# Layer 2 as one loop of 64 state steps, with the products of a step shared out anew among four engines

## What is computed

```
xn = layernorm(x)
# s: selective state space; inner width 256, 16 states
x_main, z = split(xn @ W_in.T);  x_main = silu(conv3(x_main) + conv_b)
dt_raw, B, C = split(x_main @ W_x.T)          # 64, 16, 16 columns
dt = softplus(dt_raw @ W_dt.T + b_dt);  A = -exp(A_log)
h_t = exp(dt_t * A) * h_(t-1) + dt_t * B_t * x_t;   y_t = sum_n C_t[n] * h_t[n]
s = layernorm((y + x_main * D) * silu(z) @ W_out.T + xn) * gamma + beta
# g: top 2 of 8 experts, hidden width 512
w = softmax over the best two of silu(xn @ rw1 + rb1) @ rw2 + rb2
g = xn + sum_e w[e] * (silu(xn @ we1[e] + be1[e]) @ we2[e] + be2[e])
x = x + s * silu(g)
```

## Time and profile before

| what | value |
|---|---|
| runs | median 1634.34 us of 3 (1630.02 to 1634.79) |
| profiled execution | 1637.49 us, its span 1635.7 us |
| layer 2, all four samples | 538.7 us (853.1 to 1391.8 us) |
| busy share of the whole span | TensorE 77%, weight loads 53%, VectorE 65%, ScalarE 44%, GpSimd 37% |
| mean granted clock of TensorE | 0.885 |

### The profile page before, as it was taken

One profiled execution on the slowest core, in us unless ns is written; L12 is line 12 of the kernel. 1 busy time (PEld: TensorE's weight loads), 2 busy tenths in 40 slices (PEclk: granted clock), 3 DMA queues, 4 the chain that ended last, 5 costly groups with the idle time before them and its releaser, 6 DMA issues. The chain is left out here.

```text
span 1635.7 us, 21776 instructions
## 1 busy us (share of the span) xinstructions
PE 1261.6 (77%) x7188; PEld 859.3 (53%) x7188; DVE 1070.3 (65%) x2581; ACT 724.0 (44%) x1526; POOL 599.8 (37%) x597
## 2 busy tenths in 40 slices
PE   1799999998997764666768865976784885888985
PEld 0345564554554653544564652653553554666664
DVE  1266767678786353565556995995997798634444
ACT  0255545544544243333236745653671672343322
POOL 1243344443348533332201441442343244225551
PEclk9999999999999787777787997898797798799998
DMA  8200000000000122430000000000000000001113
GB/s 172 80 1 1 1 1 1 1 1 1 1 6 28 52 78 58 129 116 7 8 1 1 1 0 1 1 0 0 1 0 1 1 1 1 27 14 34 35 34 90
DMA packets 54315, 40.36 MB, mean 25 GB/s; under 512 B 13175, under 2 KB 46685, under 8 KB 54205
## 3 DMA queue, kind: packets, MB, share of 16 engines
q1 hardware_dynamic: 35516, 23.91, 5.0%
q0 software_dynamic: 4544, 9.32, 2.1%
q10 hardware_dynamic: 14146, 5.75, 1.7%
HBM read 25.92 MB, written 13.04 MB: 24 GB/s over the span
## 5 line engine op out<-in xcount | busy, mean ns | idle before, releaser
L762 POOL TENSOR_TENSOR PR<-PR,R 128x256 f32<-128x256 f32 (+3 forms) x128 | 160.9, 1258 | 270.8 <-DVE R L1216 266.0
L1637 POOL TENSOR_TENSOR SA<-SA,H 128x512 f32<-128x512 f32 x64 | 81.6, 1275 | 258.4 <-DVE H L1864 258.4
L1859 DVE TENSOR_TENSOR_SCAN H<-DAS,H 128x512 f32<-128x512 f32 x128 | 174.2, 1399 | 0.0
L415 PEld LDWEIGHTS banks<-we,HH 128*128 128x128 f32 x1024 | 147.3, 214 | 10.3
L415 PE MATMUL banks<-BCR,identR 96*128 96x512 f32 x256 | 110.9, 520 | 53.9 <-DVE H L1864 44.3
L1033 ACT ACTIVATE PR<-banks,NM 128x129 f32<-128x129 f32 (+3 forms) x256 | 132.5, 526 | 43.7 <-DVE NM L1193 42.8
L415 PE MATMUL banks<-we,HH 128*128 128x128 f32 x1024 | 146.4, 297 | 0.0
L415 PEld LDWEIGHTS banks<-PTS,V 128*64 128x64 f32 x1280 | 73.0, 144 | 99.1 <-issue 90.6
L415 PE MATMUL banks<-XNT,we 128*128 128x512 f32 x256 | 120.7, 594 | 0.0
L415 PE MATMUL banks<-PTS,V 128*64 128x128 f32 x1280 | 105.4, 296 | 16.3 <-DVE PTS L1201 9.4
L1201 DVE COPY PTS<-banks 128x128 f32<-128x128 f32 (+3 forms) x128 | 62.2, 486 | 80.9 <-PE banks L903 78.5
(11 more groups left out here) (516 smaller groups left out, 2665.3 us busy)
## 6 DMA issues: line engine op xcount, KB each, us to landing
xsort<-zrow SPq DMA_DIRECT2D x1, 3072.0 KB, 13.1
XS<-xsort SPq DMA_DIRECT2D x12, 256.0 KB, 2.9
ysort<-PTS SPq DMA_DIRECT2D x12, 256.0 KB, 2.2
pj_stage<-in_L_ffn_w_proj SPq DMA_DIRECT2D x1, 2048.0 KB, 9.9
we<-in_L_ffn_we SPq DMA_DIRECT2D x1, 2048.0 KB, 9.6
we<-yrows SPq DMA_DIRECT2D x8, 256.0 KB, 5.0
X<-in_L_attn_resid_pre ACTq DMA_DIRECT2D x4, 256.0 KB, 4.6
xrows<-XN SPq DMA_DIRECT2D x4, 256.0 KB, 2.3
```

The costliest lines, as they stand in the source:

```text
L415: return nc.tensor.matmul(o, l, r, start=start, stop=stop)
L762: nc.gpsimd.tensor_tensor(p, p, R[:, n, :].unsqueeze(2).to_broadcast([P, 2, w]), ALU.mult).then_inc(pn, 1)
L1637: nc.gpsimd.tensor_tensor(Y[m], Y[m], H[:, n % 2, m, :], ALU.add).then_inc(ya, 1)
L1859: nc.vector.tensor_tensor_scan(H[:, n % 2, m, :], DA[:, n % 4, m, :], H[:, n % 2, m, :], 0.0, ALU.mult, ALU.add).then_inc(scn, 1)
```

## The change

`layer2()` is called once. Its loop goes over k = 0 to 63, with sample b = k // 16 and state n = k % 16.

- B and C rows: SP stores a sample's 32 rows to a DRAM tensor `rowsd` and, for each step, loads one B row and one C row spread over 128 partitions (BR, CR: three SBUF buffers each). TensorE's `rows` and the split BCR are gone.
- B products of both halves are on GpSimd (`inputs(k + 1)`, one step ahead); H has three buffers. VectorE keeps the scans and the C products, whose second input is now CR in SBUF.
- The y sum: half 0 is still GpSimd's addition (`add_y`); half 1 is summed in PSUM bank 1 by TensorE (`sum_y`, a product with the identity). D times x_main opens the sum: on GpSimd for half 0, by a diagonal matrix DD on TensorE for half 1.
- The convolution is on TensorE: three products of shifted XT with W_in weights that are scaled by each tap (WJ, made once in layer 2 by two VectorE products from a row that SP spreads by a transfer of 3 KB to each partition).
- The correction of the softplus is on GpSimd (1024 columns, two instructions), and so are all three products and sums with the gate (gamma, beta, X).
- All PSUM results of the fronts and ends (transposes, router, convolution, dbc, dt, z, choice weights, biases, output projection) share bank 0, in the order of `uses`: each waits until the one before has been read. They are placed in the steps by `front_order`: sample b + 1's front runs in steps 2 to 14 of sample b, sample b - 1's end in steps 0 to 4.
- HH, the experts' silus, has one set of four buffers where it had two; `chunk` sums an expert's outputs hidden block by hidden block.
- The barriers between samples are gone; one stands behind the loop.

```diff
+        rowsd = nc.dram_tensor("rowsd", (B, 32, S), F32).ap()
...
-        def layer2(b):
-            X = X4[:, b, :, :]
...
+        def layer2():
...
+            NK = B * NS
...
+            front_order = {4: (("xnt",),), 5: (("r1",),), 6: (("logits",),), 7: (("c", 0), ("c", 1)), 8: (("dbc",),),
+                           9: (("dt", 0), ("dt", 1)), 14: (("wT",),)}
...
+                        def store_rows(b):
+                            sp.wait_ge(m0, read("dbc", b))
+                            sp.dma_start(rowsd[b], DBC[64:96, :]).then_inc(rowd, 16)
+                        def load_rows(k):
+                            b, n = divmod(k, NS)
+                            if n == 0:
+                                sp.wait_ge(rowd, 16 * (b + 1))
+                            if k >= 3:
+                                sp.wait_ge(bm, 2 * (k - 2))
+                            sp.dma_start(BR[:, k % 3, :], rowsd[b, n:n + 1, :].to_broadcast([P, S])).then_inc(rb[k % 3], 16)
+                            if k >= 3:
+                                sp.wait_ge(hc, 2 * (k - 2))
+                            sp.dma_start(CR[:, k % 3, :], rowsd[b, NS + n:NS + n + 1, :].to_broadcast([P, S])).then_inc(rc[k % 3], 16)
+                        store_rows(0)
+                        for k in range(NK):
+                            b, n = divmod(k, NS)
+                            if n == 12 and b + 1 < B:
+                                store_rows(b + 1)
+                            load_rows(k)
...
+                        def correction(b):
+                            g.wait_ge(dte, b + 1)
+                            if b >= 2:
+                                g.wait_ge(bm, 2 * NS * (b - 1))
+                            t = DTX[:, b % 2, :, :]
+                            plink(nc.gpsimd.tensor_scalar(t, E, 1.0, -1.0, ALU.add, ALU.add))
+                            nc.gpsimd.tensor_tensor(t, E, t, ALU.subtract).then_inc(cor, 1)
+                        def inputs(k):
+                            b, n = divmod(k, NS)
+                            g.wait_ge(rb[k % 3], 16 * (k // 3 + 1))
+                            if n == 0:
+                                g.wait_ge(dtx, b + 1)
+                            if k >= 3:
+                                g.wait_ge(ya, k - 3 + (k - 3) // NS + 2)
+                                g.wait_ge(yc, k - 2)
                             for m in range(2):
...
+                                nc.gpsimd.tensor_tensor(H[:, k % 3, m, :], DTX[:, b % 2, m, :], BR[:, k % 3, :],
+                                                        ALU.mult).then_inc(bm, 1)
+                        def add_y(k):
+                            b, n = divmod(k, NS)
+                            if n == 0:
+                                g.wait_ge(m0, read("c", b, 0))
+                                if b:
+                                    g.wait_ge(yz, 2 * b)
+                                nc.gpsimd.tensor_tensor(Y0, XM[:, 0, :], Dp[:, 0:1].to_broadcast([P, S]), ALU.mult).then_inc(ya, 1)
+                            g.wait_ge(hc, 2 * k + 1)
+                            g.wait_ge(ya, k + b + 1)
+                            nc.gpsimd.tensor_tensor(Y0, Y0, H[:, k % 3, 0, :], ALU.add).then_inc(ya, 1)
+                        def gates(b):
+                            g.wait_ge(gs, b + 1)
+                            if b:
+                                g.wait_ge(xo, b)
+                            nc.gpsimd.tensor_tensor(GG, GS, gamma[:, :].unsqueeze(1).to_broadcast([P, T, D]), ALU.mult)
+                            plink(nc.gpsimd.tensor_tensor(GB, GS, beta[:, :].unsqueeze(1).to_broadcast([P, T, D]), ALU.mult))
+                            nc.gpsimd.tensor_tensor(GB, GB, X4[:, b, :, :], ALU.add).then_inc(gp, 1)
...
+                        scales(0)
+                        correction(0)
+                        inputs(0)
+                        for k in range(NK):
+                            b, n = divmod(k, NS)
+                            if k + 1 < NK:
+                                inputs(k + 1)
+                            add_y(k)
+                            if n == 1 and b:
+                                gates(b - 1)
+                            if n == 2 and b + 1 < B:
+                                scales(b + 1)
+                            if n == 3 and b:
+                                out_scales(b - 1)
+                            if n == 10 and b + 1 < B:
+                                correction(b + 1)
+                        gates(B - 1)
+                        out_scales(B - 1)
...
+                            elif kind == "c":
+                                m = key[2]
+                                if b == 0 and m == 0:
+                                    pe.wait_ge(wj, 2)
+                                    pe.wait_ge(dd, 1)
+                                for j in range(3):
+                                    last = mm(o, WJ[:, m, j, :], XT[:, b % 2, j:j + S], start=j == 0, stop=j == 2)
...
+                        def sum_y(k):
+                            b, n = divmod(k, NS)
+                            if n == 0:
+                                pe.wait_ge(m0, read("c", b, 1))
+                                if b:
+                                    pe.wait_ge(yz, 2 * b)
+                                else:
+                                    pe.wait_ge(dd, 2)
+                                mm(PS[:, 1, :], DD[:, :], XM[:, 1, :], start=True, stop=False)
+                            pe.wait_ge(hc, 2 * k + 2)
+                            mm(PS[:, 1, :], ident[:, :], H[:, k % 3, 1, :], start=False, stop=n == NS - 1).then_inc(yc, 1)
...
+                        for k in range(NK):
+                            for i in range(2):
+                                chunk(2 * k + i)
+                            if k:
+                                sum_y(k - 1)
+                            for key in spare_at[k][:1]:
+                                spare(key)
+                            for i in range(2):
+                                if 2 * k + 4 + i < 4 * NE * B:
+                                    hidden(2 * k + 4 + i)
+                            for key in spare_at[k][1:]:
+                                spare(key)
+                        sum_y(LAST)
...
+                        def decays(k):
+                            b, n = divmod(k, NS)
+                            if n == 0:
+                                act.wait_ge(dts, b + 1)
+                            if k == 0:
+                                act.wait_ge(wj, 2)
+                            if k >= 4:
+                                act.wait_ge(scn, 2 * (k - 3))
+                            for m in range(2):
+                                nc.scalar.activation(DA[:, k % 4, m, :], DT[:, b % 2, m, :], ACT.Exp,
+                                                     scale=Aneg[:, m, n:n + 1]).then_inc(ex, 1)
...
+                        def dt_sums(b):
+                            d = DT[:, b % 2, :, :]
+                            v.wait_ge(cor, b + 1)
+                            v.wait_ge(m0, read("dt", b, 1))
+                            link(nc.vector.tensor_tensor(d, d, DTX[:, b % 2, :, :], ALU.add))
+                            v.wait_ge(dtl, b + 1)
+                            nc.vector.tensor_tensor(d, d, E, ALU.add).then_inc(dts, 1)
+                            v.wait_ge(dts, b + 1)
+                            v.wait_ge(m0, read("c", b, 1))
+                            nc.vector.tensor_tensor(DTX[:, b % 2, :, :], d, XM[:, :, :], ALU.mult).then_inc(dtx, 1)
+                        def scans(k):
+                            b, n = divmod(k, NS)
+                            for m in range(2):
+                                v.wait_ge(bm, 2 * k + m + 1)
+                                v.wait_ge(ex, 2 * k + m + 1)
+                                h = H[:, k % 3, m, :]
+                                nc.vector.tensor_tensor_scan(h, DA[:, k % 4, m, :], h, 0.0, ALU.mult, ALU.add).then_inc(scn, 1)
+                        def outs(k):
+                            v.wait_ge(rc[k % 3], 16 * (k // 3 + 1))
+                            for m in range(2):
+                                v.wait_ge(scn, 2 * k + m + 1)
+                                h = H[:, k % 3, m, :]
+                                nc.vector.tensor_tensor(h, h, CR[:, k % 3, :], ALU.mult).then_inc(hc, 1)
...
+                        def gated(b):
+                            v.wait_ge(m0, read("z", b, 1))
+                            v.wait_ge(ya, (NS + 1) * (b + 1))
+                            nc.vector.tensor_tensor(ZS[:, 0, :], ZS[:, 0, :], Y0, ALU.mult).then_inc(yz, 1)
+                            v.wait_ge(yc, NS * (b + 1))
+                            nc.vector.tensor_tensor(ZS[:, 1, :], ZS[:, 1, :], PS[:, 1, :], ALU.mult).then_inc(yz, 1)
...
+                        stats_in(0)
+                        v.wait_ge(wr, 16)
```

(57 more changed lines are left out.)

539 lines of the change are left out of this document (289 added, 250 removed).

## The result

The changed kernel takes 1650.7 us (median of four runs, 1648.65 to 1652.37) where the kernel before takes 1633.05 us beside it: ratio 1.011, 95% interval 1.0087 to 1.0132. That is some 18 us slower, a little under half of the 36 us that were forecast. The profiled execution took 1648.65 us with a span of 1646.8 us and a mean granted clock of 0.886 (0.885 before).

A forecast was written before the change was run, and what follows sets the result against it. VectorE was taken to bound the old steps, turns with GpSimd the new: prologue 39, steps 438, fronts 33, ends 24, start of y 4, stalls 21, tail 15 make 574 us against 538.7; forecast 1670 us, range 1627 to 1712.

The forecast's parts named there:

- The mechanism: In the steps, a VectorE instruction reading two SBUF tiles and a GpSimd instruction exclude each other, whichever started first.
- the signs named: Profile after: scan median 1.8 to 2.3 us, C products 1.0 to 1.8, GpSimd products 1.5 to 2.4, step 6.7 to 7.2.
- the signs of being wrong: Scans at 1.2 to 1.4 us, steps near 4 to 5, or GpSimd waiting for row transfers or TensorE's sums.
- The step: Plain step of GpSimd's three and VectorE's four instructions in turns: 6.85 us, bounds 6.7 and 7.2; 64 steps 438 us.
- no exclusion: Rival: in the steps both engines share after all, VectorE bounds at 4.0 us a step; 1455 us, chance 0.06.
- dear hand-overs: Rival: each alternation in the steps costs half of what it now gains, 7.6 us a step; 1720 us, chance 0.08.
- tight packing: Rival: exclusion holds, every hand-over in the steps gains and the stalls vanish; 1632 us, chance 0.17.
- stalls: Waits at steps 0 and 7 and in VectorE's routing: 7 us a sample, 21 us in all (0 to 36).
- Between the steps: Fronts, ends and stalls placed in the loop beside the plain steps: +82 us.
- The correction on GpSimd: Softplus correction, 1024 columns twice, in prologue and fronts: TENSOR_SCALAR 1.5 us and TENSOR_TENSOR 2.5, together 4.0.
- Ahead and behind: Prologue ahead of the first scan 39 us (36 to 42), tail behind the steps 15 us.
- The rival of TensorE's bursts: Some 12 us of TensorE work in steps 4 to 9, through one bank, delays the sums; 1705 us, chance 0.09.

The follow-up runs named there:

- the four altered kernels: The changed kernel with B products on VectorE (ratio 0.983), half 1's y sum on GpSimd (1.041), C products reading PSUM (0.977), or memsets for B products (0.941).
- 1.07 us more of turns in a step: The changed kernel with the y sum of half 1, and its start, on GpSimd instead of TensorE: ratio 1.041, 1700 us.
- 1.04 less: The changed kernel with C products reading a PSUM bank instead of CR and TensorE's half 1 y sums left out: ratio 0.977, 1596 us.
- everything together: The changed kernel with B products, correction and gate products on VectorE, correction and dt sums one step later, two bank reads one step earlier: ratio 0.9616, 1570 us.

## Why the prediction was right and where it was wrong

*The mechanism, right.* Two SBUF inputs on VectorE and a reading GpSimd instruction take turns. The steps of the four altered kernels came out as the theory had them before each run, within 0.02 us, and with the mechanism the sign is right. Of the signs named, scan (median 2.22 us), C product (1.13) and GpSimd product (1.85) lie in their ranges, and the step (6.56) just below its own. One of the signs of being wrong showed in small: GpSimd waits 12.2 us in all for TensorE's sums, at steps 9 and 10.

*The step, over-sized: 6.85 a step, measured 6.56.* This is the step of the prediction that failed, 64 x 0.29 = 18.5 of the miss. The working gave 6.7 with every hand-over gained and 7.0 with GpSimd's instructions in a row, and took the middle. The timeline of the plain steps shows that neither engine runs two long ones in a row while the other waits, except the C products: with three buffers of H the order settles into one alternation and stays there. And a GpSimd turn between two scans costs 1.07, less than the 1.13 that the earlier trace rows gave for one; so 6.56 lies below what was called the lower bound. Only the addition's turn took the 1.13 that was reckoned. Of the rivals, no exclusion (a step of 4.0) and dear hand-overs (7.6) are ruled out; tight packing was the nearest to the truth in its steps (6.7) and wrong in its stalls. The result lies halfway between its 1632 us and the forecast.

*Between the steps, nearly right: 82 forecast, 495.6 - 64 x 6.56 = 75.7 measured.* It is right only as a sum. The correction on GpSimd was taken as 4.0 us (1.5 + 2.5), and the groups by form show 3.65 + 2.34 = 6.0:

```profile
L1700 POOL TENSOR_SCALAR DTX<-EW 128x1024 f32<-128x1024 f32 x4 | 14.6, 3648 | 48.3 <-ACT EW L1903 48.3
L1701 POOL TENSOR_TENSOR DTX<-EW,DTX 128x1024 f32<-128x1024 f32 x4 | 9.4, 2342 | 0.3
...
L402 DVE TENSOR_SCALAR XN<-X,mv,rstd 128x128 f32<-128x128 f32 x16 | 14.1, 939 | 0.0
```

The TENSOR_SCALAR lies outside its range of 0.95 to 2.1: no row showed one so wide, and a memset and two half-wide products were poor neighbours. Of the 75.7 us, 42 are step 11 of three samples (21.4 + 21.6 + 19.0 less 3 x 6.56), where the sum had 7.6 a sample for the correction and the dt sums, and 7 of stalls for the whole sample. Elsewhere less was paid: a sample's end alone costs 9.9 us beyond its plain steps (sample 3), a front alone 18.6 (sample 0, 14.8 of them in step 11), and where both stand in one sample 27.0 and 24.3, less than their 28.5. What the sum added up as turns and stalls follows one chain in steps 7 to 11: with 1.07 us more of turns in a step their total moved from 47.8 to 47.4 us, with 1.04 less to 45.2, where the turns alone make 5.

*Ahead and behind.* Forecast 39 and 15, measured 43.2 and 15.0. Of the 4 us too few ahead of the steps, 2 are the correction's price (6.0 for 4.0). What stands ahead of it was under-sized more: ScalarE's exponential ends 31.8 us into the layer where it ended after 25.0 in the kernel before, +6.8, where the sum had +3 for the row and +3 for the turns in the bank, less 4 for the convolution. What follows the correction is 2.5 us shorter than it was.

*The rival of TensorE's bursts had a real part.* Its place was right (the shared bank, at step 7), its reason was not: it isn't the length of TensorE's work but that TensorE waits for a read that stands late in VectorE's stream. It was given 0 to 5 us a sample within the stalls. Moving the two reads gains 21 us in all (17 in the loop).

In the layer the misses are 495.6 - 520 = -24.4 in the loop, +4.2 ahead and 0 behind, together -20 us; the forecast was 1670 and the result 1650.7. (The sum of 574 less 538.7 is 35.3, not 36, and GpSimd's three were taken as 1.25 where the row has 1.275; neither matters.)

## What to carry to other kernels

Before work is moved from VectorE to GpSimd, count the instructions of both that read SBUF with two operands on VectorE's side; where that sum is longer than either engine's own, it is the step, and moving one instruction from VectorE (0.6 us a product) to GpSimd (1.03) makes it longer although VectorE had been the bound. Operands in PSUM, or work on TensorE and ScalarE, shorten it. And in an order written by hand, put each read of a shared bank at the first step at which its data is there: the price of a late one isn't at the read but in the chain that it holds up, here at step 11.

## What the runs showed of the hardware that was not expected

- In the plain steps of the changed kernel, where both engines always have an instruction ready, they alternate, and an instruction that has waited is 0.05 to 0.2 us shorter in its turn than alone: GpSimd's 128x512 product 1.03 to 1.13 (1.275 alone), a product on VectorE 0.52 to 0.6. No hand-over cost anything that could be seen.
- They do not alternate everywhere. In the kernel with everything together GpSimd's addition came at 979.96 us while VectorE ran its instructions back to back, and three more of them (two B products and a scan) went ahead before it had its turn. Which engine goes next in such a case isn't explained by these runs.

```profile
979.96 3.93 POOL L1704 TENSOR_TENSOR SA<-SA,H 128x512 f32<-128x512 f32 x1 [7.72 <-DVE H L2033]
980.40 1.28 DVE L2017 TENSOR_TENSOR H<-DTX,BR 128x512 f32<-128x512 f32 x2
981.61 3.36 DVE L2026 TENSOR_TENSOR_SCAN H<-DA,H 128x512 f32<-128x512 f32 x2
```

- GpSimd's TENSOR_SCALAR with two constants over 128x1024 takes 3.65 us, more than its TENSOR_TENSOR of the same size with two inputs (2.34).
- VectorE's TENSOR_SCALAR with one SBUF tile waits for a GpSimd instruction too. Four of 128x128, 1.11 us in the earlier trace rows, took 4.00 at 1048.83 us beside two B products and an addition of GpSimd. Three of the four ended within 0.1 us behind the end of one of these; GpSimd's second and third took 1.26 us each and lost nothing. The group's mean is 939 ns. The row:

```profile
1048.83 4.00 DVE L402 TENSOR_SCALAR XN<-X,mv,rstd 128x128 f32<-128x128 f32 x4
```

 The Trainium skill lists it among those that can contend ("SBUF — State Buffer", section "Who interferes with whom"), and here the trace agrees; the scalar-tensor-tensor additions of 128x128 with one operand in PSUM keep their 1.11 for four.
- GpSimd's memset of 128x512 takes 0.49 us, and the scan and the C products beside it lose nothing.
